# A windowed-attention block with a long software pipeline: the turn of the second LayerNorm's rows moved next to the turn back

## What is computed

```
y   = layernorm(x) ; roll by (-3, -3) ; cut into windows
qkv = win @ qkv_w.T ; attn = softmax(q k^T * scale + bias + mask)
x   = x + roll_back((attn v) @ proj_w.T + proj_b)
z   = layernorm(x, norm2_w, norm2_b)
out = x + gelu(z @ fc1_w.T + fc1_b) @ fc2_w.T + fc2_b
```

## Time and profile before

| | |
|---|---|
| median of 3 runs | 2223.52 us |
| profiled execution, its own time | 2220.58 us |
| its span | 2218.8 us |
| PE busy | 2154.5 us, 97% |
| POOL, DVE, ACT busy | 1770.4, 1749.5, 1546.7 us (80, 79, 70%) |
| DMA | 165.86 MB, mean 75 GB/s |

### The profile page before, as it was taken

How to read it: one execution, slowest core, us unless ns; L and a number is a source line. 1 busy time by engine, 2 the same in 40 slices (tenths; PEclk the granted TensorE clock), 3 DMA queues, 4 the chain that set the end, 5 groups by cost and what they waited for, 6 DMA issues and landing times.

```text
span 2218.8 us, 148006 instructions
## 1 busy us (share of the span) xinstructions
PE 2154.5 (97%) x62790; PEld 1668.8 (75%) x62790; DVE 1749.5 (79%) x3231; ACT 1546.7 (70%) x2435; POOL 1770.4 (80%) x1687
## 2 busy tenths in 40 slices
PE   6999999999999999999999999999999999999997
PEld 3777777777777777777777777777777777777775
DVE  5788877887887888788788878878878877887874
ACT  3576777677677777767767776776777777677675
POOL 4888888888888888888888888888888888888874
PEclk8999999999999999999999999999999999999999
DMA  4232323222323332322222323222223332323321
GB/s 109 67 76 76 74 76 74 76 76 74 77 75 75 77 74 75 74 75 75 75 77 74 75 74 76 76 75 77 73 76 76 75 75 75 76 75 75 77 68 34
DMA packets 178587, 165.86 MB, mean 75 GB/s; under 512 B 21144, under 2 KB 152458, under 8 KB 178074
## 3 DMA queue, kind: packets, MB, share of 16 engines
q1 hardware_dynamic: 178074, 157.60, 27.9%
HBM read 28.99 MB, written 25.77 MB: 25 GB/s over the span
## 4 chain that ended last, share of the span: by engine, by line
PE 83%; ACT 9%; issue 4%; SPq 1%; DVE 1%; DMA 1%; ACTq 0%; POOL 0%; DVEq 0%; POOLq 0%
PE O L758 13%; PE ST L744 10%; PE M L766 9%; PE S L722 9%; PE ST L738 8%; PE M L851 8%; PE M L829 6%; PE M L798 5%; PE M L814 5%; PE M L784 5%; ACT L445 5%; ACT gl L445 4%; PE M L859 3%; PE S L726 1%; SPq L274 1%
## 5 line engine op out<-in xcount | busy, mean ns | idle before, releaser
L326 POOL TENSOR_TENSOR nmd<-diag,nm 121x392 f16<-121x392 f16 x1024 | 898.0, 886 | 319.0 <-DVE nm L582 311.9
L582 DVE TENSOR_REDUCE nm<-S 121x8 f16<-121x392 f32 x1024 | 576.6, 563 | 272.9 <-PE S L722 149.4
L426 ACT ACTIVATE pT<-ST 113x392 f32<-113x392 f32 x1024 | 506.6, 495 | 311.1 <-PE ST L744 306.4
L758 PEld LDWEIGHTS O<-vx,pT 113*49 113x49 f32 x16384 | 546.0, 126 | 45.3 <-issue 5.5
L758 PE MATMUL O<-vx,pT 113*49 113x18 f32 x16384 | 520.2, 196 | 3.2 <-DVE on L592 1.6
L722 PE MATMUL S<-kp,qp 128*49 128x49 f16 x16384 | 388.1, 185 | 12.2 <-DVE nm L582 8.7
L738 PE MATMUL ST<-qp,kp 128*49 128x49 f16 x16384 | 385.9, 185 | 3.1 <-issue 2.8
L722 PEld LDWEIGHTS S<-kp,qp 128*49 128x49 f16 x16384 | 313.1, 103 | 84.9 <-issue 58.1
L744 PE MATMUL ST<-nmd,shiftw 121*49 121x392 f16 x2048 | 356.4, 344 | 0.3 <-POOL nmd L326 0.2
L738 PEld LDWEIGHTS ST<-qp,kp 128*49 128x49 f16 x16384 | 323.4, 103 | 11.5 <-issue 3.3
L744 PEld LDWEIGHTS ST<-nmd,shiftw 121*49 121x49 f16 x2048 | 107.9, 102 | 264.9 <-POOL nmd L326 129.9
(11 more groups left out here) (90 smaller groups left out, 3322.4 us busy)
## 6 DMA issues: line engine op xcount, KB each, us to landing
qp<-hl SPq DMA_DIRECT2D x1024, 49.0 KB
kp<-hl SPq DMA_DIRECT2D x1024, 49.0 KB
xin<-in_x SPq DMA_DIRECT2D x256, 98.0 KB
out<-res SPq DMA_DIRECT2D x256, 98.0 KB
kp<-in_c_keys SPq DMA_DIRECT2D x4, 588.0 KB, 7.0
weights<-in_c_weights SPq DMA_DIRECT2D x1, 448.0 KB, 3.6
bias_t<-spread SPq DMA_DIRECT2D x2, 73.5 KB, 2.2
shiftw<-in_c_shift SPq DMA_DIRECT2D x1, 139.0 KB
```

Source lines behind the costliest of these rows:

```text
L326: nc.gpsimd.tensor_tensor(nmd[j % LAG][:], diag[:], nm[j % LAG][:].unsqueeze(2).broadcast_to([RM, 2 * 4, N]), ALU.mult).then_inc(s_nmd, 1)
L426: nc.scalar.activation(pT[j % LAG][:].rearrange("k w h q -> k (w h q)"), ST[0:R, j % 2, 0:HK], ACT.Exp).then_inc(s_e, 1)
L582: V.tensor_reduce(nm[j % LAG][:], S[0:RM, 0:HK].rearrange("q (h n) -> q h n", n=N), AX_X, ALU.max, negate=True).then_inc(s_nm, 1)
L758: mm = MM(O[W0 * w:W0 * w + N, (4 * p + hp) * VC:(4 * p + hp + 1) * VC], pT[j % LAG][:, w, hp, :], vx[r % RING][:, window + 2 * w, hp, :], ...
```

## The change

In TensorE's body, `turn_z` is no longer the filler of slot 7, for unit i-2. It stands at the beginning of slot 0 of the next body, ahead of `turn_back`, for the same unit, which is then i-3. Slot 7 has no filler any more. The wait that `turn_z` has where no unit i-4 exists is on place_v of unit i. In VectorE's slot 0, `normalise(c, 0)` comes before `evac_zT(e)` and not behind it.

```diff
--- before.py
+++ after.py
@@ -644,10 +644,10 @@
                     if k == 0:
                         if on_chip(d):
                             ln2_sum(d, m + 2)
+                        if on_chip(c):
+                            normalise(c, 0)
                         if on_chip(e):
                             evac_zT(e)
-                        if on_chip(c):
-                            normalise(c, 0)
@@ -819,7 +819,7 @@
                 pe.wait_ge(s_z1, u + 1)
                 if on_chip(e):
                     pe.wait_ge(s_mT, e + 1)
-                else:
+                elif on_chip(a):
                     pe.wait_ge(s_vx, 2 * a + 2)
                 turn_tokens(2, z1, s_zTp)
@@ -872,6 +872,8 @@
+                    if k == 0 and on_chip(e):
+                        turn_z(e, g, i)
                     if k == 0 and on_chip(g):
                         turn_back(g)
@@ -898,8 +900,6 @@
                     if k == 6 and on_chip(c):
                         project_out(c, f)
-                    if k == 7 and on_chip(d):
-                        turn_z(d, e, a)
```

## The result

The changed kernel takes 2190.53 us (median of 4 runs, 2188.17 to 2192.11), the kernel before 2223.34 us (median of 4): a ratio of 0.9854, with a 95% interval of 0.984 to 0.9869. That is 32.8 us less; 34 less were forecast (2189 us, range 2182 to 2209).

What follows compares the result with a forecast made beforehand. TensorE's stream, busy 97% of the span, was taken to bound the kernel. Saving 0.29 us in 125 units gives 36 us, less 2 us for q and k transfer waits: 2189 us, range 2182 to 2209.

Steps and rivals of the forecast that it cites:

- The stream of TensorE: TensorE's slots 7 and 0: moving z's turn beside mT's cuts 2.09 us to 1.80, saving 0.29 us per unit.
- The tail's neighbourhood: In the kernel's tail z and mT transposes stand adjacent, 0.45 us between their starts; the same was expected in ordinary units.
- the rival with no change at 2223 us: Order of TensorE's groups is free by the skill page's rule, so the stream keeps its length; chance 0.05.
- That VectorE's order keeps the gain: VectorE's slot 0: normalising before evacuating zT leaves its sum unchanged and the result on time for scores_T of slot 1.
- result and hand-over have 0.06 us to spare: Slot 1: GpSimd goes on at 1031.26, after the result's end; TensorE's scores_T wants it at 1031.32, so nothing is lost.
- The slower rival: The result slips behind zT and normalisation; beyond 0.35 us units lengthen, at 0.5 us 19 us slower, 2242 us; chance 0.06.
- The rival of the binding hand-overs: Result or neg_max of slot 2 comes 0.1 to 0.2 us later, giving back 12 to 25 us: 2199 to 2211; chance 0.15.
- The wait at scores of slot 3: Scores of slot 3 wait for neg_max of slot 2; VectorE gains 0.20 us, so some 0.04 us is lacking.
- That the wait of the turn of y swallows it: TensorE waits at the turn of y for the GELU anyway, so the little delay at slot 3 costs nothing.
- More waits for q and k transfers: The split into high parts waits more often than 12 cases of 128; 3.5 us at worst, 2 us taken off.
- about the same: The wait of the turn of y for the GELU, 19.4 us in 85 cases, would stay as it was.

Runs made afterwards that it cites:

- e3_double_together: Changed kernel with the turn back of mT done twice, eight transposes in a row behind the four of z: 2237.3 us, ratio 1.0066.
- e4_double_apart: Changed kernel with four extra transposes of mT standing alone in slot 7 between scores_T and the shift: 2274.86 us, ratio 1.0241.
- e1_turn_only: Changed kernel without its VectorE part, zT again evacuated ahead of the first normalisation: 2221.24 us, ratio 0.9992 to the kernel before.
- e5_veps_later: Changed kernel with the small VectorE epsilon step moved from slot 1 behind neg_max of slot 2: 2185.67 us, ratio 0.9833.

## Why the prediction was right

**The stream of TensorE: right, by its own terms.** Predicted were 0.21, 0.17, 0.43, 0.45 and 0.54 us, read in the timeline after are 0.21, 0.16, 0.44, 0.44 and 0.53. Slot 7 is 0.295 us shorter, summed was 0.29. The tail's neighbourhood did carry over. e3_double_together and e4_double_apart show by themselves that neighbours set the price, with transposes of mT where the change moved those of z: four are 0.44 us among transposes and 0.75 alone. Eight in a row, and twelve in e3_double_together, leave the ordinary units as summed, and the mean granted clock of the profiled executions is 0.993 in the changed kernel and 0.994 in e3_double_together, where the kernel before has 0.996.

Where the 0.295 us come from can be read from the starts (medians over the units): 0.095 at the entry of z (0.305 us from scores_T, where the shift stands 0.21 behind it), 0.093 at its exit (the next group 0.190 us behind the last transpose instead of 0.097), 0.088 between the first two transposes of mT (0.201 us instead of 0.113), and 0.02 from the shift to O. The prediction put these pieces down to the switch between matmul and transpose. For two of them that isn't shown, as ordinary products pay them too when their weight loads are 128 columns wide. In the changed kernel, the projection of q and k (784, loads of 64*128) and the one of v (798, loads of 128*49), each behind its scores_T:

```profile
917.37 0.37 PE L738 MATMUL ST<-qp,kp 128*49 128x49 f16 x16
...
917.67 0.93 PE L784 MATMUL M<-yT,weights 64*128 64x392 f32 x4
...
919.27 0.38 PE L738 MATMUL ST<-qp,kp 128*49 128x49 f16 x16
...
919.49 1.08 PE L798 MATMUL M<-weights,yT 128*49 128x64 f32 x32
```

That is 0.30 against 0.22 us (medians 0.302 and 0.213), and the shift to O takes 0.185 us behind the first and 0.170 behind the second. So some 0.1 of the 0.295 us may belong to a wide weight load behind narrow ones and not to transposing. No run here set a wide ordinary group next to a transpose, and the cause within the boundary stays open. The rule of "Back-to-back issue gap" in the Trainium skill's page "TensorE: Matmul & The Clock Gate" has the distance of two starts set by matmul and weight load together. As the prediction read it, the place would be free; that was the rival with no change at 2223 us, and 2190.53 us rules it out.

**That VectorE's order keeps the gain: right, and more so than written.** The sum said that result and hand-over have 0.06 us to spare. e1_turn_only, which uses that up by 0.18 us, is back at 2221 us. The slower rival had its price from this very place, and its deciding point of 0.35 us of slip was set too far: a slip of 0.18 us in two units of four and 0.28 in the other two already took nearly all. Slot 1 lost 0.11 and 0.21 us by it, and slot 2 0.07 more, as neg_max of slot 2 starts 3.96 us behind the result in both kernels and so slips with it; slot 4 gave back 0.05, but for the row-end units. The rival of the binding hand-overs was summed wrongly: the forecast's 2189 us and 12 to 25 us more are 2201 to 2214 us, where 2199 to 2211 leave out the 2 us set aside.

**The wait at scores of slot 3: mis-sized, small harm.** The prediction let VectorE gain 0.20 us ahead of neg_max of slot 2, so that 0.04 us would be lacking. It gained that at neg_max of slot 1, but lost it again: line 621, a small step on 8 elements a partition, took 0.78 us instead of the 0.54 of an ordinary unit before. It ends at 922.47, and GpSimd's second nmd at 922.44. Its end hangs on GpSimd's, whose row starts from the result (919.25) and so didn't come sooner. The prediction had no term for that line. The Trainium skill's page "GPSIMD Engine Reference", section "1. Specifications", has VectorE and GpSimd share an SBUF interface, with contention when VectorE is in a 2-port mode or has two SBUF inputs; the trace agrees in that this step ends 24 to 35 ns behind an instruction of GpSimd in every one of some 110 units, in the kernel before and in the changed one (worked out from the traces), and in e5_veps_later, where it stands elsewhere, too. That it is this interface no run shows, nor in which mode the step ran. The lack was 0.16 instead of 0.04 us.

**That the wait of the turn of y swallows it: right for ordinary units,** as slots 2 and 4 show, +0.16 and -0.18, and e5_veps_later by taking the one away and getting the other back. In row-end units there is less waiting to swallow it: they gained 0.18 instead of 0.29 us, 0.11 x 32 = 3.5 us. The prediction had not told units apart.

**More waits for q and k transfers: right in kind.** The split into high parts waited for them in 12 cases before and in 29 after:

```profile
ACT hl L407 <- DMA kp<-hl: 79.8, 29, 5.0
...
PE M L766 <- ACT gl L445: 3.0, 14, 0.2
```

The view of waits of the changed kernel also shows how the wait for the GELU shrank from 19.4 us in 85 cases; "about the same" was the prediction there, and it is wrong, since scores of slot 3 took part of it over. (The view lists waits of over 0.15 us alone; by the starts some 0.11 us are left in an ordinary unit, 0.42 us from scores_T to the turn of y where 0.305 is the least.) Mean less median unit rose by 0.01 us, 1 to 2 us in all; 2 us were set aside. Sum: 125 x 0.295 = 36.9, less 3.5, less 1.5, gives 31.9 us; measured 32.8.

## What to carry to other kernels

Put transposes on TensorE next to each other: in this kernel a group that stands apart among fp16 products costs about 0.3 us more, and none of it is seen as idle time. Whether a neighbour with equally wide weight loads would save part of that is worth a trial of its own. When one engine's row is cut, list every wait within the next slots with its slack and what its producer hangs on; here the gain stood or fell with 0.06 us in another engine's queue, and the two halves of the change were worth nothing one by one. Before taking a filler away, ask what waits behind it and not only what it waits for.

## What the runs showed of the hardware

Four fp32 transposes of 128 x 113 take 0.44 us among transposes and 0.75 us alone between an fp16 group and another (e3_double_together, e4_double_apart). Behind scores_T, whose weight loads are 49 columns wide, a group with loads of 113 or 128 columns starts after 0.30 us, transposes or not, and an ordinary one with 49 after 0.21 (medians of the changed kernel and e4_double_apart). A VectorE step on 113 x 8 elements took from 0.17 to 1.07 us, as long as GpSimd's instruction beside it still ran, and ended 24 to 35 ns behind that one:

```profile
L621 DVE TENSOR_SCALAR veps<-ss 113x8 f32<-113x8 f32 x128 | 95.9, 749 | 4.4
...
L562 DVE TENSOR_SCALAR veps<-ss 113x8 f32<-113x8 f32 x128 | 57.5, 449 | 4.4
```

These are the groups by line of the changed kernel (busy us, mean ns, idle before): the same operation in two places, 749 and 449 ns in the mean, which were 544 and 320 ns in the kernel before, with nothing changed in either.
